# Shares and second projections of the third chunk, 14 planner units later in a written-out order

## The reference, cut to what matters

```
h = layernorm(x)*(1+ca) + sa                       # x: 2 x 1024 x 128
x = x + ga * attention(h)                          # 16 heads of 8, one shared k and v, causal
h = layernorm(x)*(1+cb) + sb
g = sigmoid(h @ gate_w.T); top 4 of 16 experts     # shares = topv / sum(topv)
hin, vin = h @ e_win[e], h @ e_vin[e]              # 16 experts of width 64
routed = sum_e (silu(hin) * vin * share_e) @ e_wout[e]
shared = (silu(h @ ws_in) * (h @ vs_in)) @ ws_out
x = x + gb * (shared + routed)
```

## Time and profile before

| | us |
|---|---|
| median of 3 runs | 428.38 |
| the runs | 428.33, 431.05, 428.38 |
| the profiled execution: its time | 431.06 |
| its span, first to last instruction | 429.3 |
| PE busy | 375.5 |
| DVE busy | 278.8 |
| ACT busy | 228.4 |
| POOL busy | 91.7 |
| mean granted TensorE clock | 0.944 |

### The profile page before, as it was taken

The page is one execution under the profiler, slowest core; times in us unless marked ns, Lnnn a source line. Parts: engine busy times, 40 slices in busy tenths (PEclk is TensorE's granted clock), DMA queues, the critical chain, the costliest instruction groups (busy, mean ns, idle before and its releaser), DMA issues.

```text
span 429.3 us, 6042 instructions
## 1 busy us (share of the span) xinstructions
PE 375.5 (87%) x2123; PEld 182.3 (42%) x2123; DVE 278.8 (65%) x649; ACT 228.4 (53%) x425; POOL 91.7 (21%) x123
## 2 busy tenths in 40 slices
PE   8598939879999996899989998998897999888984
PEld 7284513343346333343364433343542443235453
DVE  4579933797995887687537744897578892141464
ACT  2312517545668862454477545676584543679422
POOL 6120461080410069050054000005017000010000
PEclk9877779988999999799999999999998999899999
DMA  7361751403200900040900000000260000003200
GB/s 190 51 80 24 156 136 19 51 9 75 51 24 5 194 6 0 14 48 17 197 0 25 2 1 0 27 2 1 64 136 2 1 2 0 25 2 98 52 2 24
DMA packets 23773, 19.46 MB, mean 45 GB/s; under 512 B 6768, under 2 KB 20496, under 8 KB 23744
## 3 DMA queue, kind: packets, MB, share of 16 engines
q1 hardware_dynamic: 23328, 18.69, 21.6%
q10 hardware_dynamic: 416, 0.39, 0.3%
HBM read 11.22 MB, written 1.17 MB: 29 GB/s over the span
## 4 chain that ended last, share of the span: by engine, by line
PE 57%; DVE 21%; POOL 8%; issue 6%; ACT 6%; DMA 1%; SPq 0%; POOLq 0%; DVEq 0%; ACTq 0%
PE bank L942 53%; DVE mn L831 12%; ACT pr L681 2%; POOL xn L558 2%; POOL rstd L549 1%; ACT L681 1%; PE bank L1118 1%; DMA qa<-qp 1%; POOL sl L623 1%; PE bank L979 1%; DVE xn L758 1%; DVE stat L863 1%; ACT L685 1%; ACT sl L685 1%; DVE ka L817 1%
## 5 line engine op out<-in xcount | busy, mean ns | idle before, releaser
L831 DVE TENSOR_REDUCE mn<-bank 128x1 f32<-128x512 f32 (+3 forms) x304 | 185.7, 655 | 59.6 <-PE bank L942 59.2
L681 ACT ACTIVATE pr<-bank 128x512 f32<-128x512 f32 x288 | 160.8, 599 | 100.5 <-PE bank L942 98.4
L942 PE MATMUL bank<-ka,qa 96*128 96x128 bf16 (+3 forms) x576 | 111.9, 287 | 19.8 <-DVE mn L831 11.0
L942 PE MATMUL bank<-qa,ka 98*128 98x512 bf16 x288 | 111.1, 398 | 2.4 <-ACT pr L681 1.7
L942 PE MATMUL bank<-pr,va 128*32 128x512 f32 x576 | 80.5, 632 | 0.7 <-ACT pr L681 0.7
L942 PEld LDWEIGHTS bank<-ka,qa 96*128 96x128 bf16 x576 | 49.7, 102 | 69.3 <-DVE mn L831 33.7
L942 PEld LDWEIGHTS bank<-qa,ka 98*128 98x128 bf16 x288 | 28.5, 101 | 86.6 <-ACT pr L681 44.6
L942 PE MATMUL bank<-hT_parts,up_parts 128*128 128x512 f32 (+1 forms) x216 | 61.4, 412 | 1.9 <-DVE sl L932 1.1
L942 PEld LDWEIGHTS bank<-hT_parts,up_parts 128*128 128x128 f32 x216 | 38.5, 190 | 13.5 <-issue 3.1
L548 POOL TENSOR_SCALAR rstd<-mv 128x4 f32<-128x4 f32 (+2 forms) x9 | 2.1, 235 | 184.5 <-DVE mv L864 184.3
L623 POOL TENSOR_TENSOR sl<-sl,comb_wide 128x512 f32<-128x512 f32 x24 | 29.8, 1272 | 50.2 <-ACT sl L685 27.4
(11 more groups left out here) (140 smaller groups left out, 276.1 us busy)
## 6 DMA issues: line engine op xcount, KB each, us to landing
comb_wide<-comb_rows SPq DMA_DIRECT2D x6, 1024.0 KB, 10.1
qa<-q_marks SPq DMA_DIRECT2D x4, 768.0 KB, 5.7
qa<-qp SPq DMA_DIRECT2D x18, 128.0 KB
comb_wide<-comb_rows SPq DMA_DIRECT2D x2, 768.0 KB, 7.7
xs<-in_L_attn_x SPq DMA_DIRECT2D x4, 256.0 KB, 5.7
qa<-qp SPq DMA_DIRECT2D x12, 64.0 KB
out_x<-xs SPq DMA_DIRECT2D x3, 256.0 KB, 2.3
sl<-in_L_ffn_e_win SPq DMA_DIRECT2D x1, 512.0 KB, 7.7
```

Source lines behind the costliest of these rows:

```text
L681: act.activation(pr[:, n % NPB, g, :], s_bank[in_s[x] % NS][:, :], ACT.Exp, scale=SCALE).then_inc(s_read, 1)
L831: v.tensor_reduce(mn[:, place[u] % 2, part, h:h + n], m_bank[k % NM][:, 0:n * w].rearrange("p (n w) -> p n w", w=w), AX.X, ALU.max, negate ...
L942: return pe.matmul(out, lhsT, rhs, start=start, stop=stop, skip_group_check=True)
```

## The change

The delay between `spread` and the first `gate` of a chunk is 14 planner units plus 1.9 for each f, and 10 plus 1.0 for `LAST`. For the third chunk in order, `CHUNKS[-2]`, that is chunk 1, it becomes 28 plus 1.9. The vins follow their gates by 1.7 units, and the downs follow the last vin, so all of them are written later. No instruction is added, removed or altered.

```diff
         elif kind == "spread":
             for f in range(1, FC + 1):
-                side.append((now + (14.0 + 1.9 * f if a != LAST else 10.0 + 1.0 * f), ("gate", a, f)))
+                wait = {LAST: 10.0 + 1.0 * f, CHUNKS[-2]: 28.0 + 1.9 * f}.get(a, 14.0 + 1.9 * f)
+                side.append((now + wait, ("gate", a, f)))
         elif kind == "gate":
             vins.append((now + (1.7 if a != LAST else 0.2), ("vin", a, x[2])))
```

## The result

| | before | changed |
|---|---|---|
| median of 20 runs | 430.52 us | 436.31 us |
| lowest to highest | 428.22 to 435.10 | 431.90 to 440.95 |
| ratio, 95% interval | | 1.0125 (1.0095 to 1.0156), some 5.4 us slower |
| profiled execution: time, span | 431.06, 429.3 | 438.46, 436.7 |

Runs over 1.5% above the fastest of their kernel are not in the ratios: three of each kernel here, the profiled one of the changed kernel (2.2 us above its median) among them, and one of 506.09 us in experiment 3. I compare stretches counted from one event that lies ahead of all that moved: the shift matmul of unit 14, at 326.16 before and 328.31 after. The 2.15 between them were lost earlier, in a part that is the same in both.

What follows compares the result with a forecast made beforehand. PE and DVE were taken as near full at the vins, the tail as setting the end. Early gain, payback and tail put up_end at 417.1 against 415.57: +1.5 on 428.38 gives 429.9 us, range 425.0 to 433.4.

Steps and rivals of the forecast that it cites:

- What bounds the kernel: Whole kernel: PE and DVE near full at chunk 1's vins, a little room on PE, the start of up_end decides.
- The order worked out: Planner order by hand: chunk 1's vins 13.92 units later, its downs ahead of unit 14's oT, last chunk's gates behind unit 15's route.
- Early part: Blocks up to 63, relieved of vins and downs: pv of block 63 at 361.2, -11.4 us.
- What is paid back: Downs ahead of unit 14's oT: oT at 376.5, 2 us later; first hin +2.9; last pv 1.6 earlier.
- two bare blocks: Blocks without vins or downs: 4.47 us together, 2.24 each, subtracted between the first hin and the last pv.
- The tail at full clock: After the last pv: evac 1.13 behind, unit 15's chain 7.1, eight gates 9.6, transfer hidden; up_end at 417.1, +1.5 us.
- The tail's clock: Rival: the idle tail lowers the clock, 5 us at half speed, 2.5 us lost, giving 432.4 us; chance 0.25.
- The likeliest case: The forecast itself: last chunk's gates at 1.2 us each behind unit 15's chain, 429.9 us in all; chance 0.50.
- The anchor: Base time for the predicted difference: +1.5 us put on the median of 428.38 us.
- No stall: Rival at unit 14's oT: bank emptied in time, 1.7 us stall and 1.6 slow clock unpaid; 425.7 us, chance 0.17.
- Gates that move: Rival on POOL: chunk 1's gates run later, freeing unit 14's small instructions, -3 us, 426.9; chance 0.03.
- the zero: SP's queue: shift passes ahead of a turn, no transfer holds another, cost zero, covered by idle queues.

Runs made afterwards that it cites:

- experiment 3: Kernel before with the last chunk's gates, vins and downs behind unit 15's h2 and route, plus 29 dummy matmuls in PE's waits; ratio 1.0113.
- experiment 1: Changed kernel plus 29 dummy 128 x 128 matmuls in PE's waits from block 71 to the last h2; ratio to the kernel before 1.0049.
- experiment 2: Kernel before with only the last chunk's gates, vins and downs written behind unit 15's h2 and route; ratio 1.0118.
- experiment 4: Changed kernel with the last chunk's gates due 4 units sooner, four meant to run among unit 15's norm2 and h2; ratio to the kernel before 1.0180.
- experiment 6: Changed kernel with gated of chunk 1 written right behind its last down; ratio to the kernel before 1.0077.
- experiment 11: Changed kernel with gated of chunk 1 right behind its last down and dummy matmuls in PE's tail waits; ratio to the kernel before 1.0037.
- experiment 7: Kernel before with gated of chunk 1 written right behind its last down; ratio 0.9946.

## Why the prediction was wrong, point by point

- **What bounds the kernel: right.** PE and DVE near full at the vins, a little room behind the maxima, and the end set by the tail.
- **The order worked out: right**, each item at the step that was forecast; and POOL's and SP's lists are the same, entry for entry, in both kernels. The shares were not put off at all.
- **Early part: right, a little small.** Forecast -11.4 at the pv of block 63, measured -12.5. Blocks 56 to 58 took 3.2 each, so a vin was worth 0.78, not 0.68: the 0.68 compares with blocks of 5 maxima each, while these three hold 13 together.
- **What is paid back: right, its terms with luck.** The stall at oT is 1.69 as forecast, oT 4.37 behind the pv of block 65. Counted from the shift of unit 14, the first hin came 2.9 later (forecast 2.9) and the last pv 1.3 earlier (forecast 1.6). But the 2.9 is two misses that cancel: oT came 0.9 later, not 2.1, by the larger early gain, and from it to the first hin it took 13.28, not 12.1. Experiment 1, with the same order there and no slow clock in it, took 12.20: the clock cost 1.1 where I had put 0.5. The "two bare blocks" of 4.47 were misread: a whole one takes 2.40 (396.83 to 399.23), and from the pv of block 70 to that of 71 only one scores is left. The sum hardly suffers.
- **The tail at full clock: right.** I summed 17.4 from the last pv to up_end; the three kernels with dummies took 17.15, term by term in experiment 1: 1.14 for 1.13, 7.12 for 7.1, 8.89 for 9.2. That the transfer would be hidden and unit 15's chain end last was right too.
- **The tail's clock: the step that failed.** The likeliest case let the gates run at 1.2 us each, at full clock, and left the fall to a rival with 0.25. In the changed kernel it was at 1.2 GHz from 402 to 415.5, and the three terms took 2.00, 8.18 and 10.69. All four traced kernels with the late gates or a part of them and no dummies (changed, experiments 2, 4 and 6) lost the clock in the tail; the three with dummies kept it, and so did the tails whose gates lie as before. The reason that I gave against, that PE's gaps behind 414 left the clock alone, was weak: it says that gaps there left the clock alone, not that these would. The rival's mechanism is what happened, though in the changed kernel the clock falls ahead of the last pv, sooner than the rival had it. Its price was 2.5; the traces show 3.7, 2.0 and 2.6 for the changed kernel, experiments 2 and 6, since the chain of small steps and the last pv slow down too, not only the burst.
- **The anchor.** I put the difference on 428.38, the median of three runs. Over 20 runs the kernel before is at 430.52. The forecast's +1.5 would have been 432.0 on it. The rival's +4.0 would have been 434.5 on it, near the 436.3 measured, and outside a range that ended at 433.4.
- **No stall: half a rival.** The stall was there in every trace that didn't move gated. Taking it away is worth 0.7 to 2.3 us in the kernel before, and 0.5 (experiments 1 and 11) to 2.1 (experiment 6) in the changed one.
- **Gates that move: they don't by this change**, as forecast. Made to move, they are worth 1.5 us by the ratios and 2.8 by the medians, against the 3 forecast. On SP the shift doesn't pass ahead of a turn, as I had written: its list is unchanged, and the zero stands.

## What to carry to other kernels

Work moved out of a full stretch into a later one comes back as delay for whatever must pass it: check which chain has its items behind the moved ones, and what of the tail is written behind that chain. In an order written by one planner for several engines, an item's new place is real only on engines where something else of their own lies between; look at each engine's list before giving an item a price. A dependent chain that runs alone can cost TensorE's clock as well as its own length, so price it at both clocks, and keep independent work between its steps.

## What was not expected of the hardware

- The clock fell where PE was left with short work: in the changed kernel from 402 to 415.5, with PE busy 0.48 and 0.06 of the two microseconds ahead of it, 0.28 of the one at 404, and fully busy from 412. 29 dummy matmuls kept it at 1.00.
- The work around the shift of unit 14 is nearly the same in all 14 traces, and a stretch at 0.50 follows in eight of them, where the shift waited 2.13 to 2.34 us, and in none of the six where it waited 0 to 1.99. No rule comes of this: ahead of unit 15's shift a wait of 1.69 was followed by such a stretch in the kernel before and experiment 3, and by none in experiment 2. One is worth about 1.6 us: the block from the pv of block 54 to that of 55 took 5.75 in the kernel before and 4.12 in experiment 7. Over whole executions time and mean clock go together: of the 35 runs of the kernel before beside experiment 3 the fastest, 428.10, had 0.952 and the slowest, 436.66, had 0.933.
- A small VectorE instruction of 0.17 us takes 1.19 while GpSimd works through products of two SBUF tiles. Of three in a row the second and third each took 1.15 to 1.19 in all 12 traces without held gates, but the first anything from 0.18 to 1.30. PE's wait at the shift of unit 14 is the length of this first one plus 1.0 in every one of the 12, so whether the stretch at 0.50 follows goes with it.

```profile
323.43 0.18 DVE L842 TENSOR_TENSOR mn<-mn 128x16 f32<-128x16 f32 x1
...
323.64 1.15 DVE L847 CAST shift<-mn 128x16 bf16<-128x16 f32 x1
```

These two are the first and second in experiment 7.
